# Low-rank layers on transposed activations in groups of 512 tokens, their result kept on chip for the projections

## The reference

```python
# layer 1: x = x + this
base  = einsum('bsi,oi->bso', x, weight) + bias
low   = einsum('bsi,bri->bsr', x, a_sel)          # rank 16, one of 8 adapters
return base + scale[:, None, None] * einsum('bsr,bor->bso', low, b_sel)
# layer 2: x = x + this
base_out = einsum('bti,oi->bto', x, W) + b
lora_h   = einsum('bti,bir->btr', x, A)           # rank 16, one of 32 adapters
return base_out + einsum('btr,bro->bto', lora_h, Bm) * 2
# layer 3, its first step: three projections of the result
q, k, v = x @ Wq.T, x @ Wk.T, x @ Wv.T
```

## Time and profile before

| what | value |
|---|---|
| median of 3 runs | 2536.72 us (2536.56 to 2539.2) |
| the profiled execution's own time | 2536.5 us |
| its span, from the first to the last instruction | 2535.0 us |
| PE busy over the span | 2425.9 us, 96% |
| DVE, ACT, POOL busy | 1797.9, 1590.7, 640.9 us |
| `lora_layers`, first to last matmul | 119.5 to 294.1 us |
| first matmul of V | 305.45 us |

### The profile page before, as it was taken

How to read it: one execution, slowest core, us unless ns; L and a number is a source line. 1 busy time by engine, 2 the same in 40 slices (tenths; PEclk the granted TensorE clock), 3 DMA queues, 4 the chain that set the end, 5 groups by cost and what they waited for, 6 DMA issues and landing times. The chain is left out here.

```text
span 2535.0 us, 55787 instructions
## 1 busy us (share of the span) xinstructions
PE 2425.9 (96%) x16326; PEld 2204.1 (87%) x16327; DVE 1797.9 (71%) x3690; ACT 1590.7 (63%) x3313; POOL 640.9 (25%) x932
## 2 busy tenths in 40 slices
PE   6799899999999979999999999999999997699999
PEld 5578688888888869999999999999999997588887
DVE  5354345988999978878888788788887884544443
ACT  3122235777877778888888888888888884311111
POOL 1222121000000034444444444444444442000000
PEclk9899899999999989999999999999999999899999
DMA  6522342333333469888898888888888974756664
GB/s 223 157 71 79 127 142 88 100 108 106 104 96 103 133 217 300 290 294 300 284 296 301 283 303 290 289 305 280 300 299 282 301 266 169 271 202 216 211 213 147
DMA packets 376142, 541.56 MB, mean 214 GB/s; under 512 B 49394, under 2 KB 263090, under 8 KB 372210
## 3 DMA queue, kind: packets, MB, share of 16 engines
q1 hardware_dynamic: 303922, 316.33, 39.0%
q0 software_dynamic: 70016, 221.30, 25.4%
q10 hardware_dynamic: 2112, 2.89, 0.4%
HBM read 442.06 MB, written 98.30 MB: 213 GB/s over the span
## 5 line engine op out<-in xcount | busy, mean ns | idle before, releaser
L1601 PE MATMUL both_ps_o<-att_pt,att_v 128*128 128x128 f32 x4096 | 539.3, 275 | 0.0
L1299 ACT ACTIVATE att_prob<-att_prob,att_shift 128x544 f32<-128x544 f32 x512 | 384.3, 751 | 205.5 <-DVE att_shift L1319 195.8
L1601 PEld LDWEIGHTS both_ps_o<-att_pt,att_v 128*128 128x128 f32 x4096 | 504.0, 191 | 0.0
L1319 DVE CUSTOM_DVE_ANT_0 att_prob<-both_ps_s,att_mask 128x544 f32<-128x544 f32 x512 | 364.8, 713 | 0.0
L101 PE MATMUL both_ps_s<-att_k_hi,att_q_hi 128*128 128x272 f32 x1024 | 339.3, 331 | 4.8 <-DVE att_k_lo L1294 4.8
L1294 DVE TENSOR_TENSOR att_k_lo<-att_k_raw,att_k_hi 128x1024 fp32r<-128x1024 f32 (+1 forms) x320 | 338.6, 1058 | 1.9 <-ACT att_k_hi L1288 1.9
L1578 PE MATMUL both_ps_pt<-both_ident,att_prob 128*128 128x128 f32 x2048 | 309.2, 274 | 6.6 <-ACT att_prob L1299 5.0
L103 PE MATMUL both_ps_s<-att_k_hi,att_q_lo 128*128 128x272 f32 x1024 | 297.9, 291 | 0.0
L1477 ACT ACTIVATE att_pt<-both_ps_pt 128x512 f32<-128x512 f32 x512 | 294.4, 575 | 2.2 <-PE both_ps_s L1586 1.2
L102 PE MATMUL both_ps_s<-att_k_lo,att_q_hi 128*128 128x272 f32 x1024 | 295.3, 288 | 0.0
L1288 ACT ACTIVATE att_k_hi<-att_k_raw 128x1024 fp32r<-128x1024 f32 (+1 forms) x320 | 292.7, 915 | 0.0
(11 more groups left out here) (191 smaller groups left out, 5160.4 us busy)
## 6 DMA issues: line engine op xcount, KB each, us to landing
att_k_raw<-in_k_pages SPq DMA_DIRECT2D x1024, 128.0 KB, 4.7
q_t<-qkv_out_t SPq DMA_DIRECT2D x128, 256.0 KB, 2.3
att_q_raw<-q_t POOLq DMA_DIRECT2D x64, 512.0 KB, 7.3
o_t<-att_o POOLq DMA_DIRECT2D x64, 512.0 KB, 6.8
out_o<-o_t SPq DMA_DIRECT2D x32, 1024.0 KB, 6.1
out_inv<-inv_t SPq DMA_DIRECT2D x32, 1024.0 KB, 6.5
qkv_w_stage<-in_w_qkv SPq DMA_DIRECT2D x12, 1024.0 KB, 5.1
l_w_stage<-in_w SPq DMA_DIRECT2D x8, 1024.0 KB, 7.2
```

Of the source, the lines that this page charges most:

```text
L1299: act.activation(prob[:, b, :], prob[:, b, :], ACT.Exp, bias=shift[:, b:b + 1], scale=-1.0, accum_out=total[:, j // HK, j % HK:j % HK + 1] ...
L1319: dve.tensor_tensor_reduce(out=prob[:, b, :].rearrange("p (a n) -> p a n", a=2), in0=ps_s[:, j % 2, :, 0:HALF], in1=mask[:, j // HK, :].re ...
L1601: pe.matmul(out, v_sb[p][:, c, h * DH:(h + 1) * DH], pt_sb[:, j % OG, c, :], start=(c == 0), stop=False)
```

## The change

`lora_layers` now works on groups of 512 tokens (`GT`), four of them, on activations that stay transposed: `state` holds features by tokens. The weights are the fixed operand and 512 tokens move. A round is one layer of one group, and the eight rounds are in a table. `low_rank`, `base` and `delta` of a layer 1 round are 12, 48 and 12 matmuls of 512 columns. Layer 2 packs eight adapters into 128 rows, so a group is two halves of 256 tokens, and its `low_rank` and `delta` are 24 matmuls of 256 columns each. Bias and residual are one VectorE operation (`scalar_tensor_tensor`), and GpSimd has no part in it. An input tile is transposed once, on its way in; ScalarE copies it twice (to `state` and as the high part). The high and low parts of layer 2's result are written where `qkv` reads its operand (`xt_hi`, `xt_lo`), and `qkv` has no load, transpose or split of it. For the last residual the result is transposed back (16 tiles, kind "z"), copied by ScalarE and stored. The loop is written out. `ROUNDS` lists (layer, group); `INPUTS_TURNED` and `RESULTS_TURNED` give for a round the group whose tiles are transposed in it, one ahead of each quarter of the output features. `adapters_after(n)` is the group of round n + 1 where that round is of layer 2; `a_hi_part` waits for the adapters' load, and with `b_lo_part(g)` the count `ab_split` reaches 4 * (g + 1). `low_rank` of layer 2 waits for `ab_split` half by half. The block's end doesn't wait for the stores; `qkv` waits for them (`x_stored`) before it loads its second weight, and its first weight is loaded during `lora_layers`.

```diff
+ROUNDS = [(0, 0), (0, 1), (1, 0), (0, 2), (1, 1), (0, 3), (1, 2), (1, 3)]
+INPUTS_TURNED = {0: 1, 2: 2, 4: 3}
+RESULTS_TURNED = {3: 0, 5: 1, 7: 2}
 # SyncE (sync)
+                def load_x(t):
+                    if t >= 4:
+                        sp.wait_ge(turned, TURN_OF["x", t - 4 if t < 6 else t - 2] + 1)
+                    sp.dma_start(x_sb[:, x_buf(t), :], x_in[rows(t), :]).then_inc(x_loaded[x_buf(t)], 16)
+                def load_adapters(g):
+                    for h in range(2):
+...
+                        if g:
+                            sp.wait_ge(ab_split, 4 * g)
+                        elif h:
+                            sp.wait_ge(weights_split, FIRST_OF[W2])
+                        for s, a in enumerate(adapters):
+                            sp.dma_start(a_in[:, h, s * KC * RANK:(s + 1) * KC * RANK], i["a2"][bass.ds(a, 1)])
+                            sp.dma_start(b_in[s * RANK:(s + 1) * RANK, h, :], i["b2"][bass.ds(a, 1)])
...
+                load_adapters(0)
+                for t in range(TPG + 2, TPG + 4):
+                    load_x(t)
+                sp.wait_ge(weights_split, FIRST_OF[B1])
+                sp.dma_start(w_in[:, 0, :, :], w_next).then_inc(kept.w_loaded[0], 16)
+                for g in range(1, LG):
+                    if g < LG - 1:
+                        for t in range(TPG * (g + 1), TPG * (g + 1) + 2):
+                            load_x(t)
+                    load_adapters(g)
+                    if g < LG - 1:
+                        for t in range(TPG * (g + 1) + 2, TPG * (g + 2)):
+                            load_x(t)
+                    for t in range(TPG * (g - 1), TPG * g):
+                        store(t)
+                for t in range(NT - TPG, NT):
+                    store(t)
 # ScalarE (scalar)
+                for n in range(len(ROUNDS)):
+                    g = adapters_after(n)
+                    low_hi_part(n)
+                    turn(n, 0)
+                    if g is not None:
+                        a_hi_part(g)
+                    for c in range(KC):
+                        y_hi_part(n, c)
+                        if c + 1 < KC:
+                            turn(n, c + 1)
...
+                    if g is not None:
+                        b_hi_part(g)
 # VectorE
+                    apply_mask(n)
+                    low_lo_part(n)
+                    turn(n, 0)
+                    if g is not None:
+                        a_lo_part(g)
+                    for c in range(KC):
+                        add(n, c)
+                        y_lo_part(n, c)
+                        if c + 1 < KC:
+                            turn(n, c + 1)
...
+                    if g is not None:
+                        b_lo_part(g)
 # TensorE
+                for n in range(len(ROUNDS)):
+                    low_rank(n)
+                    for c in range(KC):
+                        turn(n, c)
+                        base(n, c)
+                        delta(n, c)
+                for t in range(NT - TPG, NT):
+                    transpose("z", t)
 # qkv
-            act.activation(xt_hi[:, :, t * P:(t + 1) * P], ps_t[t % 2], ACT.Copy).then_inc(xhi_done, 1)
-            dve.tensor_tensor(xt_lo[:, :, at], ps_t[t % 2], f32(xt_hi[:, :, at]), ALU.subtract)\
-                        if j + 2 < NT:
-                            turn_x(j + 2)
+        for p in range(2):
+            sp.wait_ge(both.x_stored[p], 16 * NT // 2)
+        sp.dma_start(w_stage[:, 1, :, :], w_all[1]).then_inc(w_loaded[1], 16)
```

More of the change, by code:

```diff
@@ L440, in _ @@
                 tiles(pe, tile)
-def lora_layers(nc, x_in, i, x_out):
-    ROWS = (NAD1 * RANK, SPT * RANK)
+FIRST_BYTES = 72256
+SBUF_END = 229376
+LG = 4
+GT = TOK // LG
+TPG = NT // LG
+HS = P // RANK
+HT = HS * SEQ
+ROUNDS = [(0, 0), (0, 1), (1, 0), (0, 2), (1, 1), (0, 3), (1, 2), (1, 3)]
+ROUND_OF = {step: n for n, step in enumerate(ROUNDS)}
+INPUTS_TURNED = {0: 1, 2: 2, 4: 3}
+RESULTS_TURNED = {3: 0, 5: 1, 7: 2}
+TURNS = [("x", t) for t in range(TPG)]
+TURNS += [("x", TPG * INPUTS_TURNED[n] + i) if n in INPUTS_TURNED else ("z", TPG * RESULTS_TURNED[n] + i)
+          for n in range(len(ROUNDS)) if n in INPUTS_TURNED or n in RESULTS_TURNED for i in range(TPG)]
@@ L466, in lora_layers @@
[L466 to L474, removed]
@@ new lines, in x_buf, with x_loads, tokens, rows @@
+        def x_buf(t):
+            return t if t < 4 else t % 2
+        def x_loads(t):
+            return 1 if t < 4 else (t - 4) // 2 + 2
+        def tokens(g):
+            return slice(g * GT, (g + 1) * GT)
+        def rows(t):
+            return slice(t * P, (t + 1) * P)
+        def in_group(t):
+            return slice(t % TPG * P, (t % TPG + 1) * P)
+        def halves(g):
+            return [slice(h * HT, (h + 1) * HT) for h in range(2)]
+        def turn_in(n, at):
+            if n in INPUTS_TURNED:
+                return "x", TPG * INPUTS_TURNED[n] + at
+            if n in RESULTS_TURNED:
+                return "z", TPG * RESULTS_TURNED[n] + at
+            return None, None
@@ L512, in lora_layers, with adapters_after @@
+        def adapters_after(n):
+            step = ROUNDS[n + 1] if n + 1 < len(ROUNDS) else (0, 0)
+            return step[1] if step[0] else None
         with nc.Block(no_gpsimd_drain=True) as block:
@@ new lines, in store @@
+                def store(t):
+                    sp.wait_ge(z_copied, t + 1)
+                    sp.dma_start(x_out[rows(t), :], x_sb[:, 2 + t % 2, :]).then_inc(both.x_stored[t % 2], 16)
+                load_x(0)
+                load_weights(A1)
+                for t in range(1, TPG):
+                    load_x(t)
+                load_weights(W1)
+                load_weights(B1)
+                for buf, src in smalls:
+                    sp.dma_start(buf[:, :], src).then_inc(small_loaded, 16)
@@ new lines, in b_hi_part, with turn @@
+                def b_hi_part(g):
+                    if g:
+                        act.wait_ge(mm_done, KC * (ROUND_OF[1, g - 1] + 1))
+                    for h in range(2):
+                        act.activation(b2_hi[:, h, :], b_in[:, h, :], ACT.Copy).then_inc(ab_hi_done, 1)
+                def turn(n, at):
+                    kind, t = turn_in(n, at)
+                    if kind == "x":
+                        take_input(t)
+                    elif kind == "z":
+                        copy_result(t)
@@ new lines, in b_lo_part, with turn @@
+                def b_lo_part(g):
+                    for h in range(2):
+                        dve.wait_ge(ab_hi_done, 4 * g + 2 + h + 1)
+                        dve.tensor_tensor(b2_lo[:, h, :], b_in[:, h, :], f32(b2_hi[:, h, :]), ALU.subtract)\
+                           .then_inc(ab_split, 1)
+                def turn(n, at):
+                    kind, t = turn_in(n, at)
+                    if kind == "x":
+                        x_lo(t)
+                x_lo(0)
+                split_weights_lo(A1)
```

549 lines of the change are left out of this document (257 added, 292 removed).

## The result

The changed kernel takes 2548.59 us (median of 5 runs, 2547.32 to 2550.6) against 2536.72 us (2536.56 to 2539.2): slower by 11.9 us, ratio 1.0043 with the 95% interval [1.003, 1.0055]. Its profiled execution took 2550.6 us, the highest of the five; its span is 2549.0 us. TensorE is busy for 2414.2 us, 95% of the span, 11.7 us less than before. So there is less work for TensorE, and more time.

What follows compares the result with a forecast made beforehand. The prediction took TensorE's instruction stream to bound lora_layers. Stage +21.3, seam -3.2 and V part -6.6 summed to +11.5 on 2536.5, so 2548 us, with a range of 2538 to 2561 meant to hold 8 times in 10.

Steps and rivals of the forecast that it cites:

- first matmul: Start of lora_layers: TensorE's first matmul at about 118 us, up to 1.5 us earlier than before.
- TensorE's work in the rounds: Eight rounds of lora_layers: 134 us of matmuls plus 9.1 us for 24 tile transposes.
- wait for tile 6, 10, 14: Rounds 0, 2, 4: TensorE waits 6.6, 13.4 and 13.4 us for input tiles queued behind 32 adapter loads on SyncE.
- wait for down matrices, for tile 8: Rounds 6 and 7: TensorE waits 6.1 us for group 3's second-half adapters, then 4.3 us for a result tile.
- restarts at the half clock: After the four long waits and the start, matmuls run at 1.2 GHz: five times 2.1 us, 10.5 us.
- last matmul: End of lora_layers' rounds: predicted at 315.4 us against 294.1 before, the stage longer by 21.3 us.
- seam, against before: From the rounds' last matmul to the first V matmul: 8.2 us instead of 11.4, 3.2 gained.
- V part, against before: V steps in qkv lose their transposes: 14 steps at 0.47 us less each, 6.6 us gained.
- 256 columns: Layer 2's low_rank and delta matmuls: taken as 0.12 us each, near a 272-column row; the skill's formula gives 109 ns.
- (1) The queue keeps up: Rival on SyncE's queue: issue step about 0.38 us or less, time under 2532, 2496 without waits and restarts; chance 0.06.
- (2) A draw: Rival: every cost at its cheap end, with issue steps of 0.44 us, gives 2537 us; chance 0.12.
- (3) Waits inside the rounds: Rival: delta waits for the low-rank mask, copy and subtraction, 8 x 1.5 = 12 us more, 2560 us; chance 0.14.

Runs made afterwards that it cites:

- e9_all_again: Changed kernel with input loads ahead of adapter loads, up matrices issued by GpSimd, down matrices loaded once their buffers are split; 2500.11 us, ratio 0.9853.
- e7_after_again: The changed kernel run once more without edits, as a measure of scatter; 2549.26 us, ratio 1.0047 to the kernel before.
- e8_results_first: Changed kernel with group 3's down matrices split behind the quarters of round 6's result, not ahead; 2542.83 us, ratio 1.0022 to the kernel before.
- e2_up_on_gpsimd: Changed kernel with the up matrices' loads issued by GpSimd instead of SyncE; 2615.09 us on the slower chip, ratio 0.9923 to the kernel before.
- e10_turns_behind: Changed kernel with each tile's transposes, copy and split behind the quarter they stood ahead of; 2557.48 us, ratio 1.0075 to the kernel before.
- e6_all: Changed kernel with inputs ahead of adapters, up matrices on GpSimd, down matrices loaded once their buffers are split; 2598.38 us on the slower chip, ratio 0.9864.

## Why the prediction was right

The forecast was 2548, the time is 2548.59. Term by term, in us:

| step | predicted | measured |
|---|---|---|
| first matmul | 118 | 117.14 |
| TensorE's work in the rounds | 134 + 9.1 = 143.1 | 145.0 |
| wait for tile 6, 10, 14 | 6.6, 13.4, 13.4 | 6.17, 12.15, 11.92 |
| wait for down matrices, for tile 8 | 6.1, 4.3 | 4.80, 3.98 |
| restarts at the half clock | 5 x 2.1 = 10.5 | 12.9 |
| last matmul | 315.4 | 314.03 |
| seam, against before | -3.2 | -3.5 |
| V part, against before | -6.6 | -6.2 |

The work is that of e9_all_again, which has the same matmuls and no waits: 264.27 less 117.18 is 147.1 with the restart at its start, and 145.0 without, at about 2.1 for that restart. The restarts are what is left of the changed kernel's 196.9 us from first to last matmul: 196.9 - 145.0 - 39.0 = 12.9, of which 10.8 (196.9 - 147.1 - 39.0) stand behind the five waits. V's end is read from ScalarE's first row of the part behind it (`qkv_squares`), 10.5 us later than before at 415.0, where the first V matmul was 16.7 later. In the profiled execution the distance then grows to its 14.1, above the medians' 11.9; e7_after_again's own has 12.6. The cause in those later stages, whose work is the same, stays open; no experiment looked there.

**The wait for tile 10, followed through.** Group 1's adapters start 3.7 us into round 2 (163.01 to 166.73; predicted 3.6). The issues are 0.50 apart as the rows said, but the gap with the read of eight numbers is 0.73 and not 1.2, and 0.19 of it is already in the step of 0.50, so the group takes 16.6 and not 17.4. The tile is there 2.8 later, as predicted. TensorE arrives 10.9 into the round (predicted 10.5, though the prediction's own five terms add up to 10.7). 0.8 and 0.4 are what the wait is shorter by.

**Size errors that cancelled.** Five waits were 4.8 us too long in the sum, the work 1.9 and the restarts 2.4 too short. There were six restarts, not five: the wait for tile 8 costs one, too. Its 3.98 us of idle time come after 2.9 us of work at the half clock behind the wait for the down matrices, and the eight matmuls behind it are at the half clock still. In e8_results_first part of that is gained when the wait goes. The start moves by 1.5 us between two executions of this kernel, and the later stages added 1.4 that no term holds. So the match to 1 us is luck, though the mechanism isn't: every wait that was forecast stood where it was forecast. The range was the honest statement.

**256 columns.** They stand 0.12 apart:

```profile
163.01 0.28 PE L102 MATMUL lora_ps_low<-lora_y_hi,lora_a_hi 128*128 128x256 f32 x1
163.13 0.28 PE L103 MATMUL lora_ps_low<-lora_y_lo,lora_a_hi 128*128 128x256 f32 x1
```

The Trainium skill, "TensorE: Matmul & The Clock Gate", "Back-to-back issue gap", has the isolated gap of such a matmul at 109 ns. It says itself that this formula has no budget for the weight loads of a stream; in this stream, with a weight load for each, the trace shows 0.12. With the section "HAM oscillation: how this bites in real kernels" of the Trainium skill (a wait for a DMA between stretches of matmuls costs a restart at the half clock as well) the trace of the changed kernel agrees: 12.9 us of restarts stand beside 39.0 of waits.

**The rivals.** (1) The queue keeps up: it doesn't, an issue takes 0.50 and not 0.38. What the time would be if it did was put at 2496, and e9_all_again, where it does, takes 2500.11. (2) A draw wanted an issue step of 0.44; the mean was 0.50, with steps of 0.43 and 0.57 in turn. (3) Waits inside the rounds: the changed kernel shows no wait for the low-rank split in front of `delta`. It was real as a risk: e2_up_on_gpsimd shows it with 1.06 us, and e10_turns_behind, where the tiles' work was moved, with 4.36.

## What to carry to other kernels

Add up what a DMA queue issues in a round, number of issues by the distance of two of them, and see what stands behind; bytes may be few (32 issues of 32 KB kept SyncE busy for 16.6 us while they moved 1 MB). A load that the bottleneck engine wants soon belongs ahead of a batch that only the next round wants, or on another engine's queue. A rearrangement that takes TensorE's work away only pays when the stage's pace is still set by TensorE: with its waits gone the new layout takes 27 us out of the stage (174.3 us from first to last matmul before, 147.1 in e9_all_again), and as first written it gave them all back, and more, as waits on a queue whose work had been hidden, with the restarts of the clock behind them.

## What the runs showed of the hardware

- A DMA of 32 KB issued by SyncE with its address from a register costs the queue 0.50 us; from GpSimd's queue 0.57 (4.52 / 8). Splitting one into two of half the size added 0.42.
- Of idle stretches of nearly one length some are followed by the half clock and some not. After 2.77 us at 149.05 matmuls stood 0.43 apart, after 2.86 us at 201.29 in the same kernel 0.24:

```profile
201.29 0.47 PE L102 MATMUL lora_ps_low<-both_xt_hi,lora_a_hi 128*128 128x512 f32 x1 [2.86 <-DVE both_xt_lo L707]
201.59 0.40 PE L103 MATMUL lora_ps_low<-both_xt_lo,lora_a_hi 128*128 128x512 f32 x1
201.83 0.40 PE L104 MATMUL lora_ps_low<-both_xt_hi,lora_a_lo 128*128 128x512 f32 x1
```

  After 2.92 us in e8_results_first the first five 256-column matmuls stood 0.12 to 0.19 apart and those from 286.29 on 0.21, at the half clock. The length of one idle stretch alone doesn't tell; why these differ wasn't tried.
- One chip ran the kernel before in 2634.4 us, two others in about 2537. The 95 us lie in the attention (1305 against 1210 us in the same kernel); why stays open. The gain of the one kernel that was tried on both held: 36.0 us on the one (e6_all), 37.2 on another (e9_all_again).
